# A transformer layer on one core: the second half's tokens normalised in transposed form, one combination of x every four steps, and the ends of the halves reordered

## The reference

```python
xn = (x - mean) / sqrt(var + 1e-5)                 # over the channels
q = transpose(xn, (2, 0, 1))                       # for every channel: 4 x 1024
prob = softmax(einsum('lnc,lmc->lnm', q, q) / 32)  # 4 x 4 for every channel
s = xn + transpose(einsum('lnm,lmc->lnc', prob, q), (1, 2, 0))
gate, up = xn @ Wg.T, xn @ Wu.T                    # 2752 wide
g = silu((silu(gate) * up) @ Wd.T)                 # 1024 wide
out = x + s * g
```

## Time and profile before

| what | us |
|---|---|
| median of 3 runs (lowest, highest) | 2513.22 (2512.47, 2515.49) |
| the profiled execution's own time | 2514.81 |
| its span, first to last instruction | 2513.0 |
| TensorE busy (matmuls) | 2414.7 |
| VectorE, ScalarE, GpSimd busy | 1604.2, 1006.6, 84.5 |
| mean granted TensorE clock | 0.985 of full speed |

### The profile page before, as it was taken

The page is one execution under the profiler, slowest core; times in us unless marked ns, Lnnn a source line. Parts: engine busy times, 40 slices in busy tenths (PEclk is TensorE's granted clock), DMA queues, the critical chain, the costliest instruction groups (busy, mean ns, idle before and its releaser), DMA issues.

```text
span 2513.0 us, 30203 instructions
## 1 busy us (share of the span) xinstructions
PE 2414.7 (96%) x11214; PEld 1108.0 (44%) x11214; DVE 1604.2 (64%) x2751; ACT 1006.6 (40%) x1144; POOL 84.5 (3%) x72
## 2 busy tenths in 40 slices
PE   2889999999999989999999999999999999999999
PEld 1434444444444434444444444444444444444444
DVE  8888777668988857788877886656422432431431
ACT  8876777777778424444454521110000000000001
POOL 0000000000000000000000000000010011001011
PEclk7899999999999999999999999999999999999999
DMA  6856675657766795556655644229767766777764
GB/s 241 257 199 203 197 225 193 212 170 264 239 235 215 267 323 191 189 201 209 221 182 183 208 176 145 107 102 367 301 244 314 307 270 269 298 287 290 302 261 163
DMA packets 171854, 579.51 MB, mean 231 GB/s; under 512 B 17632, under 2 KB 42896, under 8 KB 153916
## 3 DMA queue, kind: packets, MB, share of 16 engines
q1 hardware_dynamic: 136716, 289.21, 33.9%
q10 hardware_dynamic: 34992, 288.37, 29.9%
HBM read 388.76 MB, written 188.75 MB: 230 GB/s over the span
## 4 chain that ended last, share of the span: by engine, by line
PE 87%; DVE 4%; issue 3%; DMA 3%; ACT 2%; SPq 0%; POOL 0%; ACTq 0%; POOLq 0%; DVEq 0%
PE ps L1764 55%; PE ps L1910 31%; DMA arena<-in_x 1%; ACT arena L760 1%; PE ps L1837 1%; PE ps L1721 1%; DMA arena<-xnsc 1%; DMA arena<-in_dn 1%; DVE arena L1291 0%; ACT arena L773 0%; DVE arena L1380 0%; DMA arena<-in_gu 0%; DVE arena L1223 0%; DVE arena L1433 0%; DVE arena L1312 0%
## 5 line engine op out<-in xcount | busy, mean ns | idle before, releaser
L1764 PE MATMUL ps<-arena 128*128 128x512 f16 x7152 | 1562.8, 381 | 34.5 <-ACT arena L966 11.3
L1764 PEld LDWEIGHTS ps<-arena 128*128 128x128 f16 x7152 | 701.7, 98 | 883.0 <-issue 19.4
L1910 PE MATMUL ps<-arena 128*128 128x512 f16 x3696 | 797.9, 379 | 0.3 <-issue 0.3
L760 ACT ACTIVATE arena<-arena,bias_t 128x2048 f32<-128x2048 f32 (+3 forms) x288 | 525.0, 1829 | 86.6 <-DMA arena<-in_dn 77.5
L1910 PEld LDWEIGHTS ps<-arena 128*128 128x128 f16 x3696 | 361.6, 98 | 436.6 <-issue 0.8
L1380 DVE TENSOR_TENSOR arena<-arena 128x512 f16<-128x512 f32 x364 | 243.1, 683 | 9.8 <-ACT arena L918 8.5
L1178 ACT ACTIVATE arena<-arena,e_d 128x512 f32<-128x512 f32 x48 | 34.6, 721 | 424.3 <-DVE arena L1686 219.4
L966 ACT ACTIVATE arena<-ps,gate_back 128x512 f32<-128x512 f32 x84 | 57.2, 681 | 301.7 <-PE ps L1764 301.5
L729 POOL TENSOR_TENSOR arena<-arena 128x512 f32<-128x512 f32 x64 | 82.5, 1297 | 2414.5 <-DMA arena<-in_xt 2106.1
L976 ACT ACTIVATE arena<-arena,gate_back 128x512 f32<-128x512 f32 x84 | 60.5, 720 | 179.1 <-DVE arena L1550 166.2
L1662 DVE SCALAR_TENSOR_TENSOR arena<-arena,sc 128x512 f32<-128x512 f32 x192 | 129.8, 743 | 0.0
(11 more groups left out here) (109 smaller groups left out, 1158.1 us busy)
## 6 DMA issues: line engine op xcount, KB each, us to landing
isc<-arena SPq DMA_DIRECT2D x308, 256.0 KB, 2.4
arena<-wdsc ACTq DMA_DIRECT2D x28, 2816.0 KB, 10.1
arena<-isc ACTq DMA_DIRECT2D x28, 2816.0 KB, 18.0
arena<-xnsc SPq DMA_DIRECT2D x48, 1024.0 KB, 8.5
wsc<-arena ACTq DMA_DIRECT2D x21, 1792.0 KB, 6.9
arena<-in_x SPq DMA_DIRECT2D x48, 512.0 KB, 6.0
arena<-in_gu ACTq DMA_DIRECT2D x43, 512.0 KB, 4.6
wdsc<-arena SPq DMA_DIRECT2D x77, 256.0 KB, 2.1
```

The lines of the kernel that those rows point to most:

```text
L760: a_.activation(buf, src, ACT.Prelu, bias=bias_t[:, i:i + 1], scale=scale, alpha=alpha).then_inc(ramps, 1)
L1764: ins = t_.matmul(ps[:, bank, :], wreg[:, b, w, wa, k, :], xreg[:, j, o, k, xa, :], start=start and (k, wa, xa) == (0, 0, 0), stop=stop an ...
L1910: ins = t_.matmul(ps[:, bank, :], ring_w[b][:, k, wa, g, :], ring_i[b][:, k, xa, :], start=first and (k, wa, xa) == (0, 0, 0), stop=r not ...
```

## The change

In words: (1) The tiles of the second half are no longer loaded again, normalised and transposed. Means and inverse roots, 8 tiles at a time, are copied along a row of 128 (`wide_rows`, VectorE), transposed by TensorE (`row_group`, four transposes each, bank 7) and copied by ScalarE (`row_copy`), so that they lie along the free dimension in all partitions: at step 8 for part j = 0 and at step 24 for j = 1. The fourth row stays in bank 7. (2) The x jobs load the transposed input `xt`, which has the channels in the partitions, normalise it with four operations on 128x1024 (`normalise`), store it to `xnsc`, and combine it; there is one at steps 10, 14, ... 38, and all high parts are casts of ScalarE. (3) There are four staging slots in place of six up to step 39, and p6 keeps bank 6 up to step 39. (4) ScalarE does sil_a ahead of c_high 5 and, in step 3, of w_high; the codes of tile 4 are loaded within step 4 and its ramps run at the end of that step. (5) Behind a remainder step, its p2 comes after p1 and p6 of the next step and its gating moves with it. The remainder's weights lie in slots 4 and 1; slot 0 is reloaded at step 41 and slot 4 at step 43. The codes of tile 23 are loaded at step 42 in place of step 44.

The core of the diff:

```diff
@@ halves
-    if s > 2:
-        out += half(s - 1, SECOND, SECOND_REST)
-    return out
+    behind = half(s - 1, SECOND, SECOND_REST) if s > 2 else []
+    if out and STEPS[s - 1][1] == LAST:
+        return out[:2] + behind + out[2:]
+    return out + behind
...
-ROOTS_AT = 8
-NORM_AT = {8 + 2 * i: (16 + 2 * i, 17 + 2 * i) for i in range(8)}
-XJOB_AT = {s: (2 + i // 4, i % 4) for i, s in enumerate([s for s in SPARE if s >= 24][-8:])}
+ROWS_AT = {8: 0, 24: 1}
+ROWS_BEHIND = ["p5", "p2", "p4", "p3"]
+XJOB_AT = {s: (2 + i // 4, i % 4) for i, s in enumerate(s for s in SPARE if s >= 10 and not PASS[s][1])}
...
-NSLOT = 6
+NSLOT = 4
...
+X_ITEMS = ["n0", "n1", "n2", "n3"] + ACT_ITEMS
+X_CUT = [0, 2, 4, 5, 9, 11, 15]
...
-    return 3 if s == 0 else 6 if s < 24 else 6 + s % 2
+    return 3 if s == 0 else 6 if s < 40 else 6 + s % 2
@@ sync, load_blocks and the step
-                sp.dma_start(blk[:, r, :, :], xnsc[tp // 2, kp + 4 * r, :, 2 * (tp % 2):2 * (tp % 2) + 2, :]).then_inc(blk_in[r], 16)
+                sp.dma_start(blk[:, r, :, :], xt[tp // 2, kp + 4 * r, :, 2 * (tp % 2):2 * (tp % 2) + 2, :]).then_inc(blk_in[r], 16)
...
+                    if c[0] == "x":
+                        sp.wait_ge(n_made, 4 * x_number(c) + 4)
+                        for r in (0, 1):
+                            sp.dma_start(xnsc[c[1] // 2, c[2] + 4 * r, :, 2 * (c[1] % 2):2 * (c[1] % 2) + 2, :], blk[:, r, :, :]).then_inc(x_stored[r], 16)
@@ scalar, reloads
-                    load_w(0, 4, 7)
+                    load_w(0, 0, 1)
+                    load_w(0, 5, 7)
...
-                    load_w(0, 0, 1)
+                    act.dma_start(wflat[:, wbuf(1, 0), 4, :, :], wsc[0, :, 4, :, :]).then_inc(w4_in, 16)
@@ scalar, the step
-                if s in DOWN_AT and DOWN_AT[s][1] == 0 and DOWN_AT[s][0] + 1 < NDOWN:
+                if s in DOWN_AT and DOWN_AT[s][1] == 0 and 0 < DOWN_AT[s][0] < NDOWN - 1:
                     load_codes(NU + DOWN_AT[s][0] + 1)
+                if s == 42:
+                    load_codes(NU + 1)
...
+                if s == 4:
+                    load_codes(4)
...
-                if late:
+                if late and s != 4:
                     ramps_of(s, 0, 2)
-                if half_tile_at(s, "p5"):
-                    evac(*half_tile_at(s, "p5"))
+                if job and job[0] == "x":
+                    for o in (0, 4, 1, 2):
+                        c_high(job, o)
+                if late and s != 4:
+                    ramps_of(s, 2, 3)
+                if s in ROWS_AT:
+                    row_copy(ROWS_AT[s], 0)
+                if s > 2:
+                    sil_a(s - 1)
+                if s in ROWS_AT:
+                    row_copy(ROWS_AT[s], 1)
                 if job:
                     c_high(job, 5)
-                if late:
-                    ramps_of(s, 2, 3)
                 if s == 3:
                     w_high(2, 6)
-                if s > 2:
-                    sil_a(s - 1)
...
-                ramps_of(s, 3 if late else 2, 4)
+                ramps_of(s, 0 if s == 4 else 3 if late else 2, 4)
+                if s in ROWS_AT:
+                    row_copy(ROWS_AT[s], 2)
@@ vector
+            def normalise(c, i):
+                n, a = x_number(c), i % 2
...
+                row = rows[i] if i < 3 else ps[:, 7, :]
+                v_.tensor_tensor(blk[:, :, a, :], blk[:, :, a, :], row.unsqueeze(1).to_broadcast([P, 2, CH]),
+                                 ALU.subtract if i < 2 else ALU.mult).then_inc(n_made, 1)
...
+                for n, src in enumerate((mv[:, 8 * k:8 * k + 8, 0:1], y[:, 1, 8 * k:8 * k + 8].unsqueeze(2))):
+                    v_.tensor_copy(wide[:, n, :, :], src.to_broadcast([P, 8, P])).then_inc(wide_made, 1)
...
-                if s == ROOTS_AT and slot == 1:
-                    dve.wait_ge(xn_act, len(NORM_ACT))
-                    dve.wait_ge(stat, 64)
-                    roots()
-                if s in NORM_AT and slot >= 4:
-                    normal(NORM_AT[s][slot - 4])
+                if s in ROWS_AT and slot == 0:
+                    if not ROWS_AT[s]:
+                        dve.wait_ge(xn_act, len(NORM_ACT))
+                        dve.wait_ge(stat, 64)
+                        roots()
+                    wide_rows(ROWS_AT[s])
@@ tensor
+            def row_group(k, g):
+                pe.wait_ge(wide_made, 2 * k + 2)
+                if g:
+                    pe.wait_ge(rows_in, 3 * k + g)
+                elif k:
+                    pe.wait_ge(n_made, 16 * k)
+                for i in range(4):
+                    ins = t_.transpose(ps[:, 7, i * P:(i + 1) * P], wide[:, g // 2, 4 * (g % 2) + i, :], id32[:, :])
+                ins.then_inc(rows_done, 1)
```

More of the change, by code:

```diff
@@ L111 @@
 JOB = {c: i for i, c in enumerate(JOBS)}
-ACT_JOB_AT = {s: jobs_at(s)[0] for s in range(8, 40) if jobs_at(s) and (PASS[s][1] or s not in XJOB_AT)}
+ACT_JOB_AT = {s: jobs_at(s)[0] for s in range(8, 40) if jobs_at(s)}
 ACT_JOBS = list(ACT_JOB_AT.values())
@@ L371, in build @@
         e_lo = sem("e_lo")
+        wide_made = sem("wide_made")
+        rows_done = sem("rows_done")
+        rows_in = sem("rows_in")
+        n_made = sem("n_made")
+        x_stored = [sem("x_stored0"), sem("x_stored1")]
         blk_in = [sem("blk_in0"), sem("blk_in1")]
@@ L626, in _ @@
                     load_scl(w, 1)
-                if s in NORM_AT:
-                    for tt in NORM_AT[s]:
-                        load_nat(tt)
-                if s + 1 in XJOB_AT and s not in XJOB_AT:
+                if s + 1 in XJOB_AT:
                     for r in (0, 1):
@@ L1082, in _ @@
                     p1_copy(s)
-                if job:
+                if job and job[0] == "i":
                     c_high(job, 0)
@@ L1519, in first_half @@
                 background(s, 1)
+                if s > 2 and STEPS[s - 1][1] == LAST:
+                    second_half(s - 1)
                 if u != LAST:
@@ L1754, in need @@
                         loads = u // 2 + 1
[L1755 removed]
+                        if u == 0 and w == REST_W[0]:
+                            pe.wait_ge(w4_in, 16)
+                        else:
+                            pe.wait_ge(w_in[b][1 if w in (1, 2, 3) else 0], 32 * loads - (16 if u == LAST else 0))
                     if u == 0:
```

117 lines of the change are left out of this document (62 added, 55 removed).

## The result

Seven runs of each kernel gave a median of 2505.39 us after (2501.68 to 2507.20) and 2513.22 before (2512.13 to 2515.49): a ratio of 0.9965, 95% interval 0.9953 to 0.9976. The kernel is faster by 7.8 us, 0.31%. Faster was forecast at 0.89; the time lies 2.4 us above the range of 2478 to 2503, and the gain is a third of the 22.7 us forecast.

What follows compares the result with a forecast made beforehand. TensorE, busy 96% of the span, was taken to bound the kernel. The terms -14.1 - 5.0 - 16.7 + 5 + 6.1 + 2 gave -22.7 us, 2490.5 us against the median of 2513.22; range 2478 to 2503.

Steps and rivals of the forecast that it cites:

- The count of groups and what each held: Steps 9 to 23: 128 transposes in 32 groups, each holding TensorE 0.44 us, go: -14.1 us.
- the four waits for evacuations: Steps 9 to 23: TensorE's four waits for a half tile's evacuation go, with their clock loss: -5.0 us.
- the three waits for sil_a in the start-up: Waits of 4.16, 5.18 and 2.00 us go, but VectorE's lateness brings some 9 us back in steps 4 and 5.
- step 24: Second row group waits 2.6 us for ScalarE's first row copy; with clock 1.7 and groups 1.8, +6.1 us (bounds 1.8, 9).
- Copies with a broadcast source: VectorE's row copies at step 8 charged 0.81 us each, the one-source price; bounds 0.6 and 1.22.
- Steps 3 to 9: VectorE's c21, roots and copies hold TensorE up; step 9 starts later than before: +5 us (bounds -8 and +8).
- The x steps: Eight steps 10, 14, ... 38: sil_a comes up to 1 us late, charged 0.25 each: +2 us (bounds 0 and 12).
- 0.4 us of slack: In an x step sil_a ends at +17.8 and is needed at 18.2; without this margin every such step pays.
- My third rival: Store waits with four slots make sil_a 2.6 us late in each of eight x steps: +10 us, 2523; 6%.
- The ends: Steps 43, 44, 45 and 87: waits of 1.65, 3.57, 7.17 and 1.65 us and clock 2.7 go: -16.7 us.
- the load of slot 1: Issued at the start of step 45, needed 10.4 us later, so charged 0 (bounds 0 and 2 us).
- Rival 4: Waits at the ends of the halves only change place; 5 of the 16.7 us gained: -11 us, 2502; 6%.

Runs made afterwards that it cites:

- slot 1 and the scales mended: Changed kernel with weight slot 1 loaded ahead of the x operands and the scales of tile 22 asked for at step 42, not 43: 2495.08 us.
- the three-fold mended kernel: Changed kernel with sil_a ahead of the x steps' casts, weight slot 1 and tile 22's scales earlier, row groups one product later: 2483.12 us.

## Why the prediction was right in sign and wrong in size

**Right.** The count of groups and what each held (32 x 0.44); the four waits for evacuations, which are absent; the three waits for sil_a in the start-up, which gave way to VectorE's c21 and to its copies; step 24, where 2.6 was forecast and 3.10 came, put down to the row copy as foreseen; the four old waits at the ends, all gone. Copies with a broadcast source took 0.69 us each, nearer to 0.81 than to 1.22 and inside the bounds. That is how the Trainium skill has it ("VectorE: DVE Perf Modes", section "The perf-mode tier table (the rule you actually need)"): one fp32 source in SBUF, twice the rate. This trace agrees, for a broadcast source too: 690 ns for 128x1024, where `normalise`, with two sources, takes 1217, and a low part with two sources 684 for half as many elements.

**Steps 3 to 9: +5 forecast, +1.5 measured.** The waits at steps 4 and 5 were 2.72 and 2.52, where I had 3.5 and 3 to 5, with one clock loss in place of two. At step 8 the copies took 0.24 less in all than charged, and the roots began at 243.3 in place of 247.1: I had carried the time of VectorE at step 8 over from before, less 1.2, though it was already 1.6 us earlier at the tile of step 4 (177.66 against 179.30) and 3.7 at one of step 6 (211.82 against 215.52). My step there was wrong by 3.8 us to the safe side.

**The x steps: +2 forecast, +12.0 measured, the step that failed.** I wrote that VectorE "is at the job about then", 7.2 us in, and that sil_a at +17.8 "just fits" 18.2. The 7.2 came from step 26 of before, whose preceding jobs had six slots and c_high 5 ahead of sil_a. I had looked for the four slots' effect only inside the x step, on c_high 3, and not in the i step before it, where c_high 5 needs a freed slot. With four slots VectorE came at +9.8, 2.6 later; less the slack of 0.4 that gives 2.2, and 2.27 was measured. With six it came at +8.2, which gives 0.6, and 0.71 was measured. With four slots and c_high 5 ahead of sil_a it came at +7.8, which gives 0.2, and no wait is listed. These fits are closer than the spread of such waits between executions, 1.4 to 2.3, allows one to rely on. The sentence that "if that 0.4 us of slack is not there, every x step pays" held for six of eight; behind steps 10 and 26 no wait stands, and the runs don't show why (in three of the kernels above a wait of 0.6 to 1.3 us stands behind step 26 too). My third rival had the right cause, four slots, but the wrong place: a wait for stores in the x step's own casts. It had 2.6 us a step, and the six waits are 1.7 on average. The cost lay at the upper bound of 12; my likeliest value, 0.25 a step, had no row of a four-slot step behind it.

**The ends: -16.7 forecast, -10.5 measured.** The term that failed is the load of slot 1, charged 0 with bounds 0 and 2; it was 4.57 and 1.6 of clock. I held 10.4 us against a landing of 7.4; the load was even issued 4 us sooner than I took it, and still landed after 19, since it queued behind 2 MB. The 7.4 was read near 600 us, in a stretch with other traffic. Rival 4 named this wait, at 6%, and put back 11.7 where 6.2 came.

**The range.** Both terms lay near or past the upper ends of their bounds (12 and 2) at once. I had summed the likeliest values and let the range hold only one such case at a time; with both at their bounds and mine elsewhere, the sum is -22.7 + 10 + 2, 2502.5, right at its end.

**What stays open**: the worth of the start-up order (some 3 to 5 us in the profiles, nothing clear in the times), why three of the four runs with slot 1 and the scales mended lie 5 us below the profiled one, and whether c_high 5 ahead of sil_a would help with six slots, which was not run.

## What to carry to other kernels

A slack read in the old kernel holds only for its history: when buffers are cut, look for the instructions that need a freed buffer, in the step before too, and at what in-order queue they stand in. Judge a load by the bytes queued ahead of it at its own place, not by the median landing of another stretch, and expect a second late load behind the first. And try small moves within a queue: three of them, each a few lines, were worth 22 us on a change whose own gain was 8.

## What the runs showed of the hardware that was not expected

The clock's answer to a wait doesn't follow its length. Behind 2.27 and 2.72 us TensorE ran at 0.78 for 7.9 us; behind 2.52 us at 1.00 (the windows above), and the 84 matmuls behind 3.10 us in the three-fold mended kernel took 18.30 us, with no loss:

```profile
161.08 18.30 PE L1830 MATMUL ps<-arena 128*128 128x512 f16 x84 [3.10 <-DVE arena L1601]
```

The 0.78 is a mean over the two levels, 1.2 and 2.4 GHz: in after, behind the 2.72 us, the granted clock is 0.50 in one stretch and nearly full in the next.

```profile
162.00:165.00 3.00, 3.00 (x8) 1.06 (x7) 2.97 (x6) 1.96 (x3) 0.00 (x0) 0.50 0.45 167
...
165.00:168.60 3.60, 3.60 (x17) 1.58 (x16) 3.39 (x5) 0.79 (x2) 0.00 (x0) 0.98 0.99 324
```

Here a row gives length, then busy us and count of TensorE's matmuls, its weight loads, VectorE, ScalarE and GpSimd, then granted clock, DMA share and GB/s. Four loads of 256 KB took 17.8 us (median) to land with the queues moving 336 GB/s, against 7.4 for stores of that size near 600 us of before. `normalise` took the same with its row in PSUM (1.21 us) as in SBUF (1.22).
